# Expert choice, ranks and indirect stores of a router moved to other places of a layer's schedule

## The reference

```python
q, k, v = (silu(conv4(x @ W.T)) for W in (Wq, Wk, Wv))
beta = sigmoid(x @ Wb.T)
delta = delta_rule(l2norm(q), l2norm(k), v, beta, chunk=32)
short, long = fir(v, 3), fir(v, 63)
paths = (short, long, delta, v)
hmid = gelu(concat(x, mean_and_var(paths)) @ gate_w1.T + gate_b1)
probs = softmax(logits(hmid) / temp); probs = max(probs, floor) / sum
out = rmsnorm(sum(probs[i] * paths[i])) @ Wo.T
x1 = layernorm(x + out)
router_logits = x1 @ router_w + router_b
weights, experts = top_k(router_logits, 2)
y = sum over the 2 experts of softmax(weights) * expert(x1)
out = layernorm(x1 + y)
```

## Time and profile before

| | |
|---|---|
| median of 3 runs | 1947.79 us |
| lowest, highest | 1944.25, 1954.17 us |
| the profiled execution, its time | 1950.38 us |
| its span in the trace | 1948.6 us |
| mean granted TensorE clock | 0.847 |
| busy: PE, DVE, ACT, POOL | 75%, 69%, 49%, 23% |
| instructions | 40303 |

### The profile page before, as it was taken

How to read it: one execution, slowest core, us unless ns; L and a number is a source line. 1 busy time by engine, 2 the same in 40 slices (tenths; PEclk the granted TensorE clock), 3 DMA queues, 4 the chain that set the end, 5 groups by cost and what they waited for, 6 DMA issues and landing times. The chain is left out here.

```text
span 1948.6 us, 40303 instructions
## 1 busy us (share of the span) xinstructions
PE 1461.2 (75%) x12217; PEld 1100.7 (56%) x12218; DVE 1352.0 (69%) x3875; ACT 948.0 (49%) x1990; POOL 443.0 (23%) x473
## 2 busy tenths in 40 slices
PE   6776075877979789789789789687419999999800
PEld 3446044746738658567467467485307777777700
DVE  6995064778878887887878888875574444444488
ACT  5771160455545654655555465432344444444434
POOL 5784200000030040130210300302042333333300
PEclk9997585987987988889879879867659999999955
DMA  5548732033253233333333332431535533333295
GB/s 190 193 162 239 185 66 52 12 74 84 58 130 97 63 103 98 88 88 108 85 100 87 110 86 66 108 98 61 168 113 162 160 94 95 96 93 95 74 368 195
DMA packets 297373, 224.36 MB, mean 115 GB/s; under 512 B 173472, under 2 KB 265632, under 8 KB 296960
## 3 DMA queue, kind: packets, MB, share of 16 engines
q1 hardware_dynamic: 225600, 158.84, 28.7%
q0 software_dynamic: 15232, 43.53, 6.2%
q10 hardware_dynamic: 56384, 19.93, 4.4%
HBM read 130.42 MB, written 91.82 MB: 114 GB/s over the span
## 5 line engine op out<-in xcount | busy, mean ns | idle before, releaser
L2019 POOL DMA_INDIRECT y_d<-C_yb,C_dest x136 | 131.6, 968 | 260.1 <-ACT C_yb L2130 257.5
L1443 DVE SCALAR_TENSOR_TENSOR B_conv<-B_ps_x,B_cw,B_conv 128x511 f32<-128x511 f32 (+2 forms) x192 | 143.4, 747 | 39.6 <-ACT B_conv L1161 34.6
L688 POOL MEMSET B_z<- 128x256 f32 (+4 forms) x40 | 5.9, 208 | 699.3 <-DMA B_z<-scr_a 699.3
L422 POOL DMA_INDIRECT xs_d<-x,slot_u x128 | 133.4, 1042 | 135.0 <-DVE m_acc L1845 98.2
L745 PE MATMUL B_ps_x<-B_xa,B_wk 128*128 128x512 f32 x128 | 86.2, 813 | 83.8 <-DVE B_sel L1435 44.9
L2255 DVE TENSOR_TENSOR C_xt_low<-C_ps_x,C_xt_high 128x256 fp32r<-128x256 f32 x136 | 57.7, 425 | 109.5 <-ACT C_xt_high L2114 109.5
L2249 DVE TENSOR_TENSOR C_av<-C_sg,C_ps_g 128x256 f32<-128x256 f32 x136 | 57.3, 421 | 95.4 <-ACT C_sg L2124 95.4
L1161 ACT ACTIVATE B_conv<-B_ps_x,B_cw 128x512 f32<-128x512 f32 x64 | 43.7, 683 | 164.0 <-PE B_ps_x L745 161.9
L2053 PE MATMUL C_ps_g<-C_w_high,C_xt_high 128*128 x272 | 119.6, 440 | 0.3 <-issue 0.3
L2053 PE MATMUL C_ps_g<-C_w_high,C_xt_low 128*128 x272 | 107.9, 397 | 0.0
L2053 PE MATMUL C_ps_g<-C_w_low,C_xt_high 128*128 x272 | 107.0, 394 | 0.0
(11 more groups left out here) (329 smaller groups left out, 4251.3 us busy)
## 6 DMA issues: line engine op xcount, KB each, us to landing
C_xb<-xs_d SPq DMA_DIRECT2D x136, 132.0 KB, 2.1
C_w_high<-y_d SPq DMA_DIRECT2D x12, 1024.0 KB, 14.2
A_band<-fir_long POOLq DMA_DIRECT2D x32, 256.0 KB, 6.1
A_work<-xT SPq DMA_DIRECT2D x16, 512.0 KB, 5.0
v_d<-A_v_tok SPq DMA_DIRECT2D x16, 512.0 KB, 3.5
short_d<-A_sh_tok SPq DMA_DIRECT2D x16, 512.0 KB, 3.2
B_xa<-xT SPq DMA_DIRECT2D x8, 1024.0 KB, 5.5
B_v_tok<-v_d SPq DMA_DIRECT2D x8, 1024.0 KB, 5.6
```

The costliest lines, as they stand in the source:

```text
L422: pool.indirect_dma_start(t["xs_d"][:, :], bass.IndirectOffsetOnAxis(ap=slot_u[:, c:c + 1], axis=0), x1[:, b, j, :], None).then_inc(done, 16)
L1443: V.scalar_tensor_tensor(conv[:, g % 2, k:], X[g % 2][:, :SEQ - k], cw[:, g // 4, gg % CH, 3 - k:4 - k], conv[:, g % 2, k:], ALU.mult, ALU ...
L2019: pool.indirect_dma_start(t["y_d"][:, :], bass.IndirectOffsetOnAxis(ap=dest[:, q:q + 1], axis=0), yb[:, u], None).then_inc(y_out[u], 16)
```

## The change

Five places are edited.

- VectorE's `choose` is split. Its first operation, the sum with the bias, becomes `route_logits` and stays in `stage1b`; the rest of `choose(i - 1)` goes into `softmax(i)`, ahead of the wait for ScalarE's exponentials. `place(i - 1)` goes from the end of `stage1b` into `merge_and_mix`, behind `taps_of(i + 2, 0)` and ahead of `merge(i + 1, 0)`. This holds for the steps 1 to 6, that is for the routing of pairs 0 to 5; pairs 6 and 7 are routed as before.
- TensorE's `rank` goes from the end of `stage1b` into `merges(i)`, behind the first merge products, where it ranks pair i - 2. `betas(i + 1)`, behind it, waits for the first operation of placing, as it overwrites what that reads. `turn_logits` has that wait in the last step only.
- TensorE's step 1 is written out, and its loop runs over 2 to 6.
- GpSimd's `mask_at(i + 1)` goes ahead of `scatter(i - 1)`.

```diff
@@ gpsimd
                 def step(i, has_prev, has_next):
                     if has_next:
                         fill_blocks(i + 1)
+                    if has_next:
+                        mask_at(i + 1)
                     if has_prev:
                         scatter(i - 1)
-                    if has_next:
-                        mask_at(i + 1)
@@ tensor
                 def betas(p):
                     need(pe, beta_ok, 2 * p)
+                    if not isinstance(p, int) or p > 2:
+                        pe.wait_ge(rt, RT * (p - 3) + 8)
                     need(pe, rn_ok, 2 * p)
@@ stage1b of tensor
                     turn_norms(p, 1)
-                    if last is not None:
-                        rank(last)
@@ merges of tensor
                         w.then_inc(m_pe, 1)
+                    if routes:
+                        rank(i - 2)
                     if has_next:
                         betas(i + 1)
@@ turn_logits of tensor
-                    if has_prev and b == 0:
+                    if not has_next and b == 0:
                         pe.wait_ge(rt, RT * (i - 1) + 8)
@@ step of tensor
-                    merges(i, has_next)
+                    merges(i, has_next, not isinstance(i, int) or i > 1)
...
                 step(0, False, True)
-                with pe.Fori(1, PAIRS - 1) as i:
+                step(1, True, True)
+                with pe.Fori(2, PAIRS - 1) as i:
                     step(i, True, True)
@@ stage1b of vector
                     if last is not None:
-                        choose(last)
+                        route_logits(last)
                     norm(p, 1)
                     if not first:
                         stats(p - 1)
-                    if last is not None:
-                        place(last)
@@ softmax of vector
                     V.tensor_tensor(lg[:], lg[:], s32[:].unsqueeze(2).to_broadcast(g3), ALU.subtract).then_inc(sm_dve, 1)
+                    if routes:
+                        choose(i - 1)
                     dve.wait_ge(sm_exp, i + 1)
@@ merge_and_mix of vector
-                    softmax(i)
+                    softmax(i, routes)
                     weigh(i, 0)
                     if has_after:
                         taps_of(i + 2, 0)
+                    if routes:
+                        place(i - 1)
                     if has_next:
                         merge(i + 1, 0)
@@ choose of vector
-                def choose(i):
-
-                    c = RT * i
-                    at = bass.ds(i * (PT * TOPK), PT * TOPK)
+                def route_logits(i):
+
                     dve.wait_ge(rt_turned, i + 1)
                     V.tensor_tensor(rl[:], TR[:, 2 * P:4 * P].rearrange("p (t r) -> p t r", r=LANE)[:, :, 0:NEXP],
                                     rb[:].unsqueeze(1).to_broadcast([P, PT, NEXP]), ALU.add).then_inc(rt, 1)
+
+                def choose(i):
+
+                    c = RT * i
+                    at = bass.ds(i * (PT * TOPK), PT * TOPK)
                     hold(dve, rt, c + 1)
@@ step of vector
                     else:
+                        route_logits(i - 1)
                         choose(i - 1)
                         stats(i)
                         place(i - 1)
-                    merge_and_mix(i, has_next, has_after)
+                    merge_and_mix(i, has_prev and has_next, has_next, has_after)
...
                 scale_norm(end)
+                route_logits(end)
                 choose(end)
                 place(end)
```

More of the change, by code:

```diff
@@ L860, in at_rest, with merges @@
                         at_products(p, AT_ORDER[k])
-                def merges(i, has_next):
+                def merges(i, has_next, routes):
                     pe.wait_ge(mt_in[0], 32 * (i + 1))
@@ L1667, in stats, with softmax @@
                     V.tensor_copy(gst[:, :, 2], gst[:, :, 0]).then_inc(st_dve, 1)
-                def softmax(i):
+                def softmax(i, routes):
                     c = 11 * i
@@ L1742, in first_rows, with merge_and_mix @@
                                     ALU.mult).then_inc(r_r, 1)
-                def merge_and_mix(i, has_next, has_after):
-                    softmax(i)
+                def merge_and_mix(i, routes, has_next, has_after):
+                    softmax(i, routes)
                     weigh(i, 0)
@@ L1793, in scale_norm @@
                     V.scalar_tensor_tensor(shift[:], mv[:, :, 0], -1.0, rstd[:], ALU.mult, ALU.mult).then_inc(ln, 1)
+                def route_logits(i):
+                    dve.wait_ge(rt_turned, i + 1)
+                    V.tensor_tensor(rl[:], TR[:, 2 * P:4 * P].rearrange("p (t r) -> p t r", r=LANE)[:, :, 0:NEXP],
+                                    rb[:].unsqueeze(1).to_broadcast([P, PT, NEXP]), ALU.add).then_inc(rt, 1)
                 def choose(i):
@@ L1798, in choose @@
                     at = bass.ds(i * (PT * TOPK), PT * TOPK)
-                    dve.wait_ge(rt_turned, i + 1)
-                    V.tensor_tensor(rl[:], TR[:, 2 * P:4 * P].rearrange("p (t r) -> p t r", r=LANE)[:, :, 0:NEXP],
-                                    rb[:].unsqueeze(1).to_broadcast([P, PT, NEXP]), ALU.add).then_inc(rt, 1)
                     hold(dve, rt, c + 1)
```

## The result

After the change the kernel takes 1986.44 us (median of 4 runs, 1982.43 to 1990.48). The kernel before took 1950.98 us beside it (4 runs, 1944.25 to 1955.34). The ratio is 1.0185, with an interval from 1.0145 to 1.0224. That is slower by 35.5 us, where 13 were forecast, and outside the range of 1948 to 1978 us.

What follows compares the result with a forecast made beforehand. No engine was taken as saturated; each stage waits for another engine. Steps 1 to 5 add 11.7 us, with step 6 13.2, less 0.2 leaves 13.0; on the median 1947.8 that gives 1960.8, or 1961 us, range 1948 to 1978.

Steps and rivals of the forecast that it cites:

- Choice into the second hole: VectorE's softmax: 3.30 us of choice fit into the 4.89 us wait for ScalarE's exponentials; gain 0, cost 0.
- Placing held by the mask: VectorE's merging, steps 1 to 5: GpSimd's mask holds placing's second operation, so TensorE's second merge product comes 2.3 us later.
- Placing out of the gate stage: VectorE's gate stage: the solver starts 1.5 us sooner, but the softmax then waits 2.4 instead of 0.93 us; gain 0.
- VectorE ... follows TensorE at +2.3: Behind the merge copy: VectorE, 2.7 us late, later waits for the last merge product, so follows TensorE's 2.3 us lateness.
- the sum of 13: Whole kernel: 11.7 us for steps 1 to 5, 13.2 with step 6, less 0.2 for TensorE's written-out step, leaves 13.0.
- Rank and beta products covered: TensorE's merging: rank (bounded by 1.0 us) and the beta products' new wait fit its 2.73 us wait; no cost.
- Step 6, the plain 1.5 us: VectorE's merging in step 6: without taps, placing is not held by the mask and costs its plain 1.5 us.
- TensorE's step 1 written out: TensorE's loop: one turn with 3.45 us idle ahead of L745 less, worth 0 to 0.6 us, taken as 0.2.
- Stores beside merging and recurrence: Sixteen indirect stores, 20.6 to 26.6 us, put x between 0.3 us early and 2.6 late; cost taken as 0.
- rival D: Stores shut VectorE out in the merging, holding some ten two-tile operations a step: 60 us, 2021; chance 0.04.
- B: Rival: the load of x behind the stores is 2.6 us late in six steps: 15.6 us more, 1976; chance 0.14.
- Rival C: Gate stage: choice and placing are on the path after all, so their removal makes the kernel faster, 1932; chance 0.1.

Runs made afterwards that it cites:

- e2_solver_late: The changed kernel with an unused VectorE reduce of 1.9 us ahead of the solver; 1966.19 us, ratio 1.01 to the kernel before.
- e1_small_mask: The changed kernel with GpSimd's mask cut to one block of 128 columns; 1966.76 us, ratio 1.0075 to the kernel before.
- e3_mask_behind: The changed kernel with GpSimd's whole mask put behind the stores; 1963.88 us, ratio 1.0076 to the kernel before.
- e10_before_later: The kernel before with an unused VectorE reduce over seven tiles ahead of the merge copy, holding it back by 1.9 us; 1979.53 us, ratio 1.015.
- e5_before_late: The kernel before with nothing moved, but an unused VectorE reduce of 1.4 us ahead of the merge copy; 1948.57 us, ratio 0.9995.
- e6_rank_turn: The changed kernel with the rank in another PSUM bank, so the beta products no longer wait for placing; 1983.94 us, ratio 1.0162 to the kernel before.
- e9_mask_then_stores: The changed kernel with placing behind the first merge copy, rank in another bank, mask ahead of the stores but after the first weighing; 1950.32 us, ratio 1.0008.
- e8: The kernel before with its mask held until the first weighing of values of the step is done; 1949.84 us, ratio 0.9996.

## Why the prediction was wrong

- **Choice into the second hole, cost 0**: right. The waits forecast were 4.3, 2.4 and 1.6 us; 4.32, 3.24 and 1.78 came.
- **Placing held by the mask, L887 2.3 us later**: right in size where it applies. L1845 took 1.44 us and L889 came 1.7 and 2.2 us later in steps 1 and 2.
- **Placing out of the gate stage, gain 0**: here the first error lies. The sum takes the mask where it was, "from 721.34 to 725.19", so that it can hold the placing alone. But the mask came 0.9 us sooner against E in step 2 and 1.2 in step 3, and in steps 3 to 5 held a 1.22 us operation to 4.85. The lateness became 4.6 us instead of 2.3, though the placing itself was then no longer held. I wrote that the solver's result "lands sooner, but ScalarE's and TensorE's next work is not waiting for that", and did not ask about GpSimd. That the sooner solver is what brought the mask is not shown: e2_solver_late puts the solver back, and the mask still comes at E + 4.2 to 5.1. e1_small_mask and e3_mask_behind take the hold away; in steps 1 to 5 of the profiled executions that is 6.7 us of the 36.0 that these steps had grown by, a change of the clock's pattern included (four late steps instead of three). I had both numbers in the earlier trace rows, the mask at 443.63 and the operation at 443.8, and read them for the placing only.
- **"VectorE ... follows TensorE at +2.3"**, and so the sum of 13: here the second error lies, and the larger one. It takes the work behind L887 to be as long as before. It is not: with L745 in another place against the clock's beat, three of five steps ran the second 64x64 product and what follows at 1.2 GHz, some 18 us by the estimate above (6.6 a step between steps 3 and 4). e10_before_later brings the same late return about in the kernel before, in four steps, by 0.55 us more of idle work than e5_before_late has. I had not read the granted clock in the merging at all, although the products of 7.08 and 4.04 us stood on the timeline I used.
- **Rank and beta products covered**: right. The new wait is 21.0 us in sum, but e6_rank_turn, which takes it away, is only 2.5 us below the changed kernel, less than either spreads.
- **Step 6, the plain 1.5 us**: right in size (L889 1.4 us later), but the step came out 1.7 us shorter, by a fall of the clock that of these two only the kernel before has in it.
- **TensorE's step 1 written out**: TensorE has four waits ahead of L745 of this kind instead of five, 13.8 us against 17.8, as forecast; its 0.2 us can't be told.
- **Stores beside merging and recurrence**: no cost, as taken. They took 23.6 us in step 2 (728.10 to 751.71), between the 20.6 and 26.6 of the prediction, single ones up to 2.0 us, and the load of x behind them held nobody. The two-tile operations beside them stayed at 1.21 to 1.24 us, so rival D has nothing for it. Nor had B: x was never late.
- **Rival C**, a shorter gate stage: no. e9_mask_then_stores has choice and placing out of it, and its steps are as long as before.

What stays open: what lets the mask's last loads through sooner, why the rise falls on its two sides with a difference of 0.1 us (127.5 us went both ways), and what e8's last stage gave back.

## What to carry to other kernels

When a change shifts TensorE's work by a microsecond or two, look at the granted clock behind the shift before summing up the shifts: if it comes back on a single large product among small ones, the step's length jumps, and a shift can cost nothing or 7 us. Test a cause by adding an unused operation of graded length to the kernel before; if the answer isn't monotonic, read the granted clock of each step before looking for another cause. And profile a step pattern more than once, or compare it with the spread of the times: one execution can have late steps that another lacks. And when a stage is freed of work, list who waits for what now comes sooner, the engines off the path too: a transfer or a mask that comes sooner can meet an operation it used to miss.

## What the runs showed of the hardware

- TensorE can be busy throughout with small products and yet be at 1.2 GHz. In step 3 of e9_mask_then_stores it was busy 3.49 of the 3.50 us from 858.0 to 861.5, with 32x32 products at a granted clock of 0.97, and then fell to 0.50. In step 2 of the changed kernel it was busy 4.00 of 4.00 us (745 to 749) and stayed at 0.50. In the steps with an early return the clock came back on the projection of 128x512.
- The time of a step is not a continuous function of a delay: 1.4, 1.9 and 3.1 us of extra delay ahead of the merge copy gave steps of 136.5, 143.4 and 140.0 us.
- A delay of 1.2 us of the first 64x64 product, ahead of the rise, cost nothing (e5_before_late, 0.9995), nor did 3.3 us saved in step 0 show in the total (e8_before_wait, 0.9996).
- The mask and a two-tile product of VectorE exclude each other by fractions of a microsecond: the mask 0.16 us ahead of the product holds it to 4.85 us; 0.2 us behind its start (721.51 against 721.30) it leaves it at 1.22 and takes 4.70 instead of 3.85 us itself. In step 0 of the ten profiled executions whose mask is the whole one and has no wait added, it starts anywhere from E + 4.3 to 4.9 against the product's E + 4.67, and holds it in seven of them.
